# Writing out the engines' hardware loops of a decoder layer as one straight program on Trainium2

## What is computed

```
x = x + self_attention(layernorm(x))        # RMS norm, 16 heads of 8, causal, softmax, Wo, plus its normed input
x = x + cross_attention(layernorm(x), ctx)  # 16 heads of 8, 1601 keys per batch, softmax, Wo
x = x + ffn(layernorm(x))                   # RMS norm, rotary attention (16 heads of 64, causal), RMS norm,
                                            # shared expert + top 3 of 31 routed experts (128 -> 128 -> 128, gelu)
```

## Time and profile before

| what | us |
|---|---|
| median of 3 runs | 1836.27 |
| lowest and highest of them | 1831.43, 1836.29 |
| the profiled execution, its time | 1832.63 |
| its span, first to last instruction | 1830.8 |
| PE busy, of the span | 1594.9 (87%) |
| DVE, ACT, POOL busy | 1126.0, 908.8, 557.7 |

### The profile page before, as it was taken

How to read it: one execution, slowest core, us unless ns; L and a number is a source line. 1 busy time by engine, 2 the same in 40 slices (tenths; PEclk the granted TensorE clock), 3 DMA queues, 4 the chain that set the end, 5 groups by cost and what they waited for, 6 DMA issues and landing times. The chain is left out here.

```text
span 1830.8 us, 34368 instructions
## 1 busy us (share of the span) xinstructions
PE 1594.9 (87%) x11045; PEld 847.1 (46%) x11045; DVE 1126.0 (62%) x2537; ACT 908.8 (50%) x1614; POOL 557.7 (30%) x690
## 2 busy tenths in 40 slices
PE   2677776699899999999899999799999998499998
PEld 1344443144444444444444444466666666344443
DVE  4755542677677685867678686456666654355564
ACT  1333333176665666666666666355555554134433
POOL 4010102030210303030111200388888886133332
PEclk9889886599999999999999999899999999599999
DMA  5222212512232323303232310000000000000001
GB/s 110 66 43 58 46 36 69 97 42 60 42 95 47 95 46 90 52 33 65 47 95 46 95 33 2 8 1 1 0 0 0 0 1 1 6 19 21 18 21 35
DMA packets 88405, 75.15 MB, mean 41 GB/s; under 512 B 24724, under 2 KB 78388, under 8 KB 87348
## 3 DMA queue, kind: packets, MB, share of 16 engines
q1 hardware_dynamic: 88276, 73.44, 18.3%
HBM read 42.73 MB, written 30.42 MB: 40 GB/s over the span
## 5 line engine op out<-in xcount | busy, mean ns | idle before, releaser
L1153 DVE TENSOR_REDUCE b_chunk_max<-psum 128x1 f32<-128x400 f32 (+1 forms) x1024 | 545.9, 571 | 217.0 <-PE psum L1368 209.1
L1291 ACT ACTIVATE b_prob<-psum 128x1024 f32<-128x1024 f32 (+1 forms) x416 | 426.0, 1024 | 256.2 <-PE psum L1405 247.5
L1368 PE MATMUL psum<-k_stack,q_stack 128*128 128x400 bf16 (+1 forms) x1024 | 321.0, 347 | 30.3 <-DMA k_stack<-b_k_scratch 11.0
L1377 PE MATMUL psum<-b_prob,b_v_aug 128*32 128x256 f32 (+1 forms) x3328 | 268.0, 394 | 2.6 <-PE psum L1320 1.7
L1405 PE MATMUL psum<-q_stack,k_stack 128*128 128x256 bf16 (+1 forms) x1664 | 255.3, 277 | 17.0 <-issue 16.7
L1405 PEld LDWEIGHTS psum<-q_stack,k_stack 128*128 128x128 bf16 (+1 forms) x1664 | 146.5, 100 | 137.9 <-issue 71.6
L1566 POOL TENSOR_SCALAR c_prob<-c_prob,c_rec 128x128 f32<-128x128 f32 (+1 forms) x256 | 193.4, 773 | 10.7 <-POOL c_kT L1575 10.1
L2049 DVE TENSOR_TENSOR e_hg<-e_gl,e_gate 128x512 f32<-128x512 f32 x128 | 128.8, 1025 | 107.9 <-ACT e_gl L2030 73.7
L1368 PEld LDWEIGHTS psum<-k_stack,q_stack 128*128 128x128 bf16 x1024 | 100.1, 98 | 200.7 <-DVE b_chunk_max L1153 170.6
L1649 DVE SCALAR_TENSOR_TENSOR c_turned<-psum,c_bias,c_tab 128x256 f32<-128x256 f32 x256 | 106.1, 476 | 110.8 <-PE psum L1782 110.8
L1684 ACT ACTIVATE c_prob<-psum,c_mneg 128x128 f32<-128x128 f32 (+1 forms) x256 | 104.3, 420 | 138.5 <-DVE c_mneg L1626 138.5
(11 more groups left out here) (213 smaller groups left out, 2021.8 us busy)
## 6 DMA issues: line engine op xcount, KB each, us to landing
k_stack<-b_k_scratch SPq DMA_DIRECT2D x32, 600.4 KB, 10.2
b_k_scratch<-b_kparts SPq DMA_DIRECT2D x7, 1200.8 KB, 4.4
b_k_scratch<-b_kparts SPq DMA_DIRECT2D x7, 800.5 KB, 6.1
b_ctx<-in_ctx SPq DMA_DIRECT2D x8, 576.0 KB
e_w<-in_L_ffn_re_w SPq DMA_DIRECT2D x62, 64.0 KB, 1.8
a_scratch<-a_parts SPq DMA_DIRECT2D x16, 192.0 KB, 2.1
k_stack<-a_scratch SPq DMA_DIRECT2D x16, 192.0 KB, 4.8
q_stack<-b_q_scratch SPq DMA_DIRECT2D x32, 96.0 KB, 2.2
```

The source lines that it names most:

```text
L1153: nc.vector.tensor_reduce(out=chunk_max[:, half, q, column4(hh), c:c + 1], in_=psum[:, 2 + u % 2, 0:w], axis=AX.X, op=ALU.max).then_inc(ma ...
L1291: nc.scalar.activation(prob[0:k, buf, :].rearrange("p (a c) -> p a c", a=2), psum[0:k, 4 + 2 * buf:6 + 2 * buf, :], ACT.Exp, scale=HD ** - ...
L1368: nc.tensor.matmul(psum[:, 2 + u % 2, 0:hi - lo], queries_of(qst, h, slice(q * P, q * P + P)), keys_of(kst, h, slice(lo, hi)), start=True, ...
L1377: last = nc.tensor.matmul(pv[32 * hh:32 * hh + 32, :], v_aug[0:k, kt, g * GH + hh, :], prob[0:k, buf, c:c + T], start=(kt == 0), stop=(kt ...
```

## The change

Each `with eng.Fori(0, n) as i:` becomes `for i in range(n):` of the Python that builds the program. So the body is emitted n times, with numbers in place of the counter register: in semaphore values, in tile addresses and in DRAM addresses of DMAs. `Tally` loses its `enter`, `leave` and the product. The other functions are unchanged, and every computing instruction and every DMA stands in the order in which it ran before.

```diff
--- before.py
+++ after.py
@@ -414,11 +414,9 @@
         def program(eng, tally, begin, attend):
 
             begin()
-            with eng.Fori(0, B // 2 - 1) as i:
-                tally.enter(i)
+            for i in range(B // 2 - 1):
                 for j in range(2):
                     attend(i * 2 + j, j, True, True)
-                tally.leave(B // 2 - 1)
             for j in range(2):
                 attend(B - 2 + j, j, j == 0, False)
 
@@ -785,27 +783,15 @@
 class Tally:
 
 
-
     def __init__(self, per):
-        self.n, self.per, self.i = dict.fromkeys(per, 0), per, None
+        self.n = dict.fromkeys(per, 0)
 
     def up(self, name, by=1):
         self.n[name] += by
         return self.now(name)
 
     def now(self, name, back=0):
-        n = self.n[name] - back
-        return n if self.i is None else self.i * self.per[name] + n
-
-    def enter(self, i):
-        self.i, self.start = i, dict(self.n)
-
-    def leave(self, rounds):
-        for name, n in self.n.items():
-            assert n - self.start[name] in (0, self.per[name]), (name, n - self.start[name], self.per[name])
-            if n != self.start[name]:
-                self.n[name] = self.start[name] + rounds * self.per[name]
-        self.i = None
+        return self.n[name] - back
 
 
 def wait(eng, sem, value):
@@ -964,11 +950,9 @@
 
             prologue()
             part(-1, 3, first=True, last=False)
-            with eng.Fori(0, B - 2) as i:
-                tally.enter(i)
+            for i in range(B - 2):
                 for r in range(4):
                     part(i, r, first=False, last=False)
-                tally.leave(B - 2)
             for r in range(4):
                 part(B - 2, r, first=False, last=False)
             for r in range(3):
@@ -1964,11 +1946,9 @@
 
             for k in range(STEPS):
                 part(None, k)
-            with eng.Fori(0, ROUNDS) as i:
-                tally.enter(i)
+            for i in range(ROUNDS):
                 for k in range(STEPS):
                     part(i, k)
-                tally.leave(ROUNDS)
 
         @block.sync
         def _(sp):
@@ -1982,8 +1962,7 @@
             load_row(slice(0, 1), 1)
 
             T_.n["y"] = 0
-            with sp.Fori(0, ROUNDS) as i:
-                T_.enter(i)
+            for i in range(ROUNDS):
                 for j in range(2):
 
                     sp.wait_ge(hg_ready, T_.up("y", WCH))
@@ -1992,7 +1971,6 @@
                     sp.wait_ge(y_done, T_.now("y"))
                     sp.sem_inc(passed, 1)
                     pre.load_expert(sp, i * 2 + 1 + j, j)
-                T_.leave(ROUNDS)
             for c in range(WCH):
                 sp.wait_ge(x_done, c + 1)
                 sp.dma_start(out.rearrange("b (q p) d -> p (b q) d", p=P)[:, c * 4:(c + 1) * 4, :], t["x"][:, c * 4:(c + 1) * 4, :])\
```

## The result

| | before | after |
|---|---|---|
| median, us | 1834.72 (4 runs, 1831.43 to 1836.29) | 1805.53 (4 runs, 1801.6 to 1805.63) |
| the profiled execution, us | 1832.63 | 1805.63 |
| its span, us | 1830.8 | 1803.6 |

The ratio is 0.9835, with a 95% interval of 0.9818 to 0.9851: the kernel is faster by 1.65%, 29.2 us by the medians and 27.0 us by the profiled executions. The forecast was 1806.

The account below looks back on a forecast made before the run. PE, busy 1594.9 of 1830.8 us, was taken to bound the kernel, losing time at the cross attention's taken branches. Terms 16.7 + 6.65 + 1.4 + 1.0 + 1.0 = 26.8 off 1832.6 gave 1806 us, range 1799 to 1815.

Parts of the forecast that it names:

- term (1): Cross attention: PE's five idle stalls at taken branches, inferred to be instruction fetches, vanish: -16.7 us.
- Could other work have filled this time: Cross attention: asked whether the stalls' loss returns later; answered no, since DVE and ACT wait for PE's scores; full 16.7 us.
- Body too long to be kept: Cross attention: body is read anew each lap, so a taken branch costs 3.58 us in the median.
- Term (2): Cross attention: PE's half clock behind the stalls goes, taken as batches' excess over batch 0 without its stall: -6.65 us.
- Term (3): Cross attention: register instructions go, -1.4 us, the middle between +1.5 (load late in each batch) and -4.4.
- Rival (A): Cross attention: in straight code the k_stack load is late in each batch; 1809 us, chance 0.08.
- Terms (4) and (5): Self attention: SP's register work before loads, -1.0 us (0 to 1.7); rotary attention: register work, -1.0 us (0 to 6).
- Term (6): Experts: registers and branches are hidden by matmuls, 0 us; the end is 3 us.
- The rule weighed: Cross attention: the skill's 108 ns per compare-and-branch would make five jumps worth 0.5 us; rejected for the trace's 16.7.
- (B): Cross attention: the wait only moves, since something at a batch's start returns without a branch; 1829 to 1833 us, chance 0.04.
- (C): Stages with short loops: straight code starves PE, 19 new packets each stalling it 3.3 us; 1869 us, chance 0.03.
- (D): More gain: rotary norm chain 6 us, cross-attention registers 4.4, self attention 1.7; 1797 us, chance 0.04.

Follow-up runs that it names:

- e5: Kernel before, cross attention still a loop with its register instructions, its jump back announced to the sequencer by a hint: 1814.72 us against 1834.54.
- e7: Kernel before, rotary loop as two laps of three batches (1914 instructions on PE): 1838.08 us against 1836.51, one run.
- e11: Kernel before, cross attention written out for PE alone, other engines keep the loop: 1834.24 us against 1834.93.
- e9: Changed kernel with 28 increments of an unused semaphore on PE ahead of cross-attention batches 1 to 5, a pause without a jump: 1833.2 us, one run.
- e6: Kernel before, rotary loop as three laps of two batches (1278 instructions on PE): 1835.8 us against 1836.51, one run.
- e8: Changed kernel with 56 increments of an unused semaphore on PE ahead of cross-attention batches 1 to 5: 1852.45 us against the kernel before's 1836.51.
- e10: Changed kernel with 128 semaphore increments on PE ahead of the cross attention's first scores, shifting PE's code against packet boundaries: 1817.49 us, one run.
- e2: Kernel before, self attention, rotary attention and experts written out, cross attention keeps its loop: 1835.44 us against 1834.54.
- e1: Kernel before, only the loop of the cross attention written out: 1808.72 us against 1834.54, ratio 0.9862.

## Why the prediction was right, and where it was not

**What bounds the kernel; term (1), five stalls, -16.7.** The place and the sum are right, and the cause is what I inferred: a fetch that the jump has to wait for (the packets behind the branches, e5, e7). Two statements around it fell.

The step "Could other work have filled this time" was answered from what DVE and ACT wait for, and not from what they do at that moment. Had PE's jump been the one thing, e11 would have gained over 20 us, and it gained nothing. DVE's own jump of 2.8 us would have held PE up just as long. The forecast survived only because the change removes both, and that was luck. What the kernel costs with a slow jump on DVE alone is shown by e11 (612.9 us for the six batches, against 614.5); a slow jump on PE alone was not run, but e9 has a pause of its size on PE alone (616.8).

"Body too long to be kept" is wrong as I put it. With the jump announced the same body stays for six laps without one packet (e5). What is lost at an unannounced jump is its beginning. My reading is that the sequencer, which does not know of the jump, reads on past the branch and overwrites the oldest code; a shorter body leaves room for both (PE's in e6 does, in e7 it does not). On PE the limit in this form lies between 1278 and 1880 instructions; on DVE between 190 (the self attention's body, whose jump is fast) and 272 (e6). The number of instructions alone does not decide: ACT jumps over 347 of them in e7 in 0.26 us. Why it does, no run shows; where a body lies against the boundaries of the packets was not varied. The Trainium skill, "Runtime: NRT & Kernel Launch", section Instruction fetch mechanics, gives buffers of 2048 instructions on PE and 512 on the others, prefetched in sequence alone, and says that a taken branch out of the window waits for a fetch. The packets behind the slow branches agree with that; by the size of the buffers alone, though, 1880 and 272 instructions would have stayed. The overwriting itself no run shows directly, but the count of packets speaks for it: 10 packets carried 1304 matmuls and as many weight loads in the earlier trace rows, 260 instructions each, so a lap of 1880 needs 7.2, and each of the four whole laps from 483.8 to 896.9 us moved 9. Each lap read more than its body.

**Term (2), the clock behind the stalls, -6.65.** Right in kind and a little small. e9 and e8 measure it without a jump: 8.6 and 9.3 us for five pauses. In the kernel before 25.35 - 16.7 = 8.65 us lie beyond the idle time, and with the next term's 1.1 taken off, 7.6 are left. I had set off each batch against batch 0, which has itself no pause at its start but registers in it.

**Term (3), registers in the cross attention, -1.4.** The sum is right, its parts were not known to me. The registers cost 2.2 us in six laps (e5, with the announced jump in it), and the late load takes some 1.1 us back: measured -1.1. Rival (A) was half true: the load is late, but only in batches 0, 2, 4 and 6, and e10 shows why. Bounding it by batch 6 alone was as far as the trace of before went.

**Terms (4) and (5), -2.0.** Not settled. By the medians e2 has nothing of them (1.0009 [0.9991, 1.0027]), while the whole change, in another session, is 3.2 us below e1. In the self attention the 0.29 us between SP's last store and its first load did shrink: timeline of SP, then of PE, after (the earlier trace rows before).

```profile
116.21 2.69 SPq L441 DMA_DIRECT2D q_stack<-a_mparts  x4
119.02 0.88 SPq L211 DMA_DIRECT2D a_q_stack<-a_scratch  x2
...
125.88 0.61 PE L750 MATMUL psum<-mask_qk,identb 128*128 128x512 bf16 x1 [3.92 <-DMA k_stack<-a_scratch]
```

It is 0.12 us now (119.02 - 118.90), and PE waits 3.92 instead of 4.21 us. That is 0.2 to 0.3 us per boundary, six of them at most 1.7 us, and below what the medians can tell. The traces of all kernels say more than one pair. Batch 0 of the cross attention starts at 379.05 to 382.25 us in the four with the self attention written out (after, e2, e8, e9; e10 has its increments there), 380.9 in the median, and at 381.89 to 387.20 in the nine with its loop, 383.4 in the median. The rotary batches 1 to 6 take 283.6 us in the median of five kernels with that stage written out (283.4 to 285.3) and 284.6 in that of seven with its loop (284.5 to 285.8). So both terms are likely there, with some 2.5 and 1.0 us, one trace per kernel, and the first could be larger than forecast.

**Term (6), the experts, 0.** Right: two experts take 13.73 us before and after. The second matmul after (the earlier trace rows before):

```profile
L2042 PE MATMUL psum<-e_hg,e_w 128*128 128x512 f32 x256 | 131.9, 598 | 8.6 <-DVE e_hg L2027 8.6
```

**The rule weighed.** The trace of before disagreed with the 108 ns that the Trainium skill, "Advanced Engine Details and Errata", section Control Flow Timing, gives for a compare-and-branch, and the runs say when: on PE a branch falls through in 67 to 83 ns and is taken in about 220 if its target is held, and takes 3.3 to 3.8 us if it is not. The estimate of 0.5 us for five jumps would have been of the right kind for e5's loop.

**The rivals.** (B), the wait only moves, is ruled out by the starts after. Yet its idea came true in e11, in a form that I had not written: another engine's wait comes in its place. (C), straight code starves PE, is ruled out: 88 packets against an expected 85, no idle "issue" on PE at a new place, and the price of the fetches is the 1.1 us of late loads. (D) gave too much to the rotary stage.

## What to carry to other kernels

A hardware loop costs next to nothing while its body is short on every engine, so look at the jump of each engine, not only of the one that bounds: in this kernel DVE and PE had slow jumps beside each other, and mending PE's alone gained nothing. The branch row is not enough for that. On PE it holds the wait (3.58 us in the median), on DVE it reads 0.06 us whether the jump is slow or fast, and only the time from the branch to the sequencer's next instruction tells. Where a jump takes microseconds, write the loop out, shorten the body, or announce the jump: the hint alone brought 20 us (1834.54 to 1814.72), with the program no longer than it was. And a pause on PE costs more than its length, since the clock is at half behind it: add some 1.7 us for each of a few microseconds.

## What the runs showed of the hardware that I had not expected

- Behind each slow jump one packet of code is moved, 1.0 to 1.4 us after the branch, and the engine goes on 1.3 to 1.5 us after its end.
- The jump back over 1880 PE instructions takes 0.22 us with the back edge announced and 3.3 to 3.8 us without; at the end of the announced loop the straight path pays for one fetch, 2.53 us of idle and 3.4 us at half clock.
- DVE's jump over 272 or 315 instructions takes 2.8 to 3.1 us, while its branch row reads 0.06; ACT's over 231 and over 347 takes 0.25.
- Pauses of 3.80 and of 8.05 us have nearly the same surcharge, 1.7 and 1.9 us each, although half clock lasts for 3.4 to 6.8 us behind the first and 6.8 to 10.2 around the second.
- A run of semaphore increments on PE takes some 0.15 us each, over twice what I had assumed.
- One packet of code, fetched among the program's own transfers, delays the last of these by 1.6 us.
